# Reciprocals on GpSimd, a second place for context rows, and earlier norms of tile 1, in a layer of windowed attention and a ternary feed-forward

## The chip, the cores and the metric

The kernel is one program that runs on all 8 cores of one Trainium2 chip. Each core has five engines with instruction streams of their own: PE (TensorE, matrix products and transposes into PSUM), DVE (VectorE), ACT (ScalarE), POOL (GpSimd) and SP (SyncE, which here only starts DMAs). They meet only in semaphores. The metric is device time in microseconds of the slowest of the 8 cores. The cores get different rows of the input and the same weights.

## The reference, cut to what matters

```python
x = x + _layernorm(attn(_layernorm(x), Wq, Wk, Wv, Wo))     # attention over 4 sinks and the last 512 keys
x = x + _layernorm(ffn(_layernorm(x), fast_b, w_fc, w_proj, u, v, gate))

def _bitlinear(x, w_latent):
    scale = clip(mean(abs(w_latent), axis=1, keepdims=True), 1e-05, None)
    tern = clip(round(w_latent / scale), -1.0, 1.0)
    w = w_latent + stop_gradient(tern - w_latent)
    return x @ (w * scale).T
h = _bitlinear(x, w_fc) + gate * (x @ v.T @ fast_b.T @ u.T)   # w_fc: 4096 x 1024
r = maximum(h, 0.0)
return _bitlinear(r * r, w_proj)                              # w_proj: 1024 x 4096
```

`x` is 2 x 16384 x 1024. The mask leaves attention only to the last 516 rows of each batch entry; all other rows pass through the feed-forward part alone. Each core has 4096 rows.

## The kernel before, in words

**Tiles.** The 4096 rows of a core are 8 tiles of 512 rows, and a tile is 4 blocks of 128 rows (i = 0 to 31). A block is normed (`stats1`, `apply1` on DVE, `rstd1` on ACT between them), transposed into `xnT`, multiplied in 32 chunks of hidden units (`fc(j, hc)` into the three PSUM banks `fcb`), put through ReLU (`relu`, ACT, makes `rpp`) and squared (`square`), and multiplied by the second weight (`proj`). From tile 2 on all squares are DVE's.

**Preparation.** Both weights are made ternary on the core while tiles 0 and 1 pass. There are 64 units of 128 x 1024: 32 of `w_fc` (n = 0 to 31) and 32 of `w_proj` (n = 32 to 63). A unit is loaded (`wload` on SP, into one of nine places, so unit n + 9 mostly follows unit n), its absolute values are summed (`abssum`, ACT), and for every four units POOL makes a threshold (`group`, writes `thr`, `hsc2`, `nthr`). `cut(n)` on DVE compares in two passes, `below` and `tern` (`ternp` for `w_proj`), and a DMA turns the result into `Sfc` or `Spj`. For a quarter of the first 32 units (`BY_PE`) PE turns it instead (`unit`) and ACT copies it out of the PSUM tile `pt` (`evac`). The low-rank term is folded into the same comparison: POOL scales `us` by the reciprocal `rthr` of the threshold into `usd`, `ut(g)` on PE turns it into `pt`, ACT copies it (`ut_copy`), and `low_rank(n)` multiplies into PSUM, where `cut(n)` reads it.

**Order.** Each engine runs a loop of its own over n = 0 to 63 that is written out by hand. In iteration n DVE cuts unit n + 2, PE does `fc(0, n - 2)` and `low_rank(n + 3)`, and ACT does `abssum(n + 8)` and the ReLU of chunk n - 3. The reciprocals are `over(g)` on DVE, in the iterations 4, 8 and so on ahead of `cut(n + 2)`. The four blocks of tile 1 are loaded after units 11, 13, 15 and 17 (`XROWS`) and normed in the iterations 25 to 28 (`STATS`). In iteration 33 PE turns the four blocks, ACT copies them (`turned`), and tile 1's 32 chunks follow (`CHUNKS`), with first halves of tile 0's products among them. `out_scale(0)` on PE stands behind the turns and in front of tile 1's chunks.

**Context rows.** In tile 2 the 645 rows of attention's context (six groups, the last of 5 rows) are normed between chunks: `ln(g)` after chunk 4g + 3, `ln_end(g)` after chunk 4g + 4. They are loaded through POOL's queue into the one tile `lrow`, so that the load of group g waits for `ln_end(g - 1)`. The same queue loads the attention's weights into two tiles `wsl`.

## Time and profile before

| | before |
|---|---|
| median of 3 runs | 1085.4 us (1084.92 to 1088.9) |
| profiled execution: its own time | 1083.28 us |
| profiled execution: span of the slowest core (core 5) | 1081.7 us |
| spans of the 8 cores | 1075.2 to 1081.7 us |
| PE busy | 1004.2 us, 93% of the span |
| DVE, ACT, POOL busy | 52%, 34%, 4% |
| DMA read from HBM, written | 87.79 MB, 17.31 MB |

The span runs from the first to the last instruction of the slowest core; the execution's own time is 1.6 us longer. PE is near its limit over the whole, so what can change is in the stretches in which it is not. All rows below are of core 5, and times in them count from the start of its span.

### The profile page before, as it was taken

Reading aid. Unit: us, or ns where it says so; the run is one execution under the profiler, and the core shown is the slowest. Engines: PE = TensorE matmul, PEld = TensorE weight load, DVE = VectorE, ACT = ScalarE, POOL = GpSimd, SP = SyncE. Lnnn points to the kernel's source line nnn. Section 1 sums busy time; section 2 is a strip of 40 time slices with the busy share of each in tenths; the row PEclk is TensorE's granted clock in tenths of the full one; section 3 lists DMA queues with packets and bytes.
Section 4 is the critical chain, followed back from the end, with each engine's and each line's share of the span. In section 5 each row is a group of like instructions: output and inputs, shape, how many; then the busy total and the mean of one; then the engine's idle time right before and its main releaser. Section 6 shows DMA issues by size and latency. Waiting matters only on the chain.

```text
span 1081.7 us, 14983 instructions; the slowest of 8 cores (1075.2 to 1081.7 us)
## 1 busy us (share of the span) xinstructions
PE 1004.2 (93%) x4933; PEld 456.6 (42%) x4933; DVE 563.5 (52%) x819; ACT 362.6 (34%) x699; POOL 39.0 (4%) x97
## 2 busy tenths in 40 slices
PE   3789769999999789999999999999999999999997
PEld 1223234444444334544544444445444444444443
DVE  4878968735555443553445344634445354544333
ACT  4779787530003431134211341123301232013200
POOL 0001011000001000000000000000000000000000
PEclk9999889999999999999999999999999999999999
DMA  8899788923553214610445123622244301311011
GB/s 268 191 241 292 188 223 204 219 60 107 146 137 102 72 37 108 162 51 8 75 108 128 47 45 78 156 59 65 46 109 138 78 21 30 113 54 40 1 64 54
DMA packets 106367, 116.93 MB, mean 108 GB/s; under 512 B 82333, under 2 KB 82589, under 8 KB 106292
## 3 DMA queue, kind: packets, MB, share of 16 engines
q1 hardware_dynamic: 102324, 103.64, 36.9%
q0 software_dynamic: 3728, 12.25, 5.9%
q8 instruction: 42, 0.69, 0.3%
q14 instruction: 33, 0.27, 0.1%
q10 hardware_dynamic: 240, 0.07, 0.0%
HBM read 87.79 MB, written 17.31 MB: 97 GB/s over the span
## 4 chain that ended last, share of the span: by engine, by line
PE 78%; DMA 7%; DVE 6%; issue 5%; ACT 3%; SPq 1%; POOL 0%; DVEq 0%; ACTq 0%; POOLq 0%
PE pjp L642 37%; PE fcb L625 28%; PE pjp L625 2%; DMA lrow<-ctx 2%; DMA Sfc<-tern 1%; PE xp L788 1%; PE xp L642 1%; PE xp L751 1%; PE fcb L642 1%; ACT rpp L1019 1%; DVE below L1426 1%; DMA r<-x 1%; DMA stg<-wpj 1%; PE pt L625 1%; ACT absd L1059 1%
## 5 line engine op out<-in xcount | busy, mean ns | idle before, releaser
L625 PE MATMUL fcb<-xnT,Sfc 128*128 128x512 bf16 x1792 | 405.8, 383 | 17.0 <-DVE r L1402 14.4
L642 PE MATMUL pjp<-Spj,r 128*128 128x512 fp8e4 x1664 | 366.8, 380 | 1.7 <-DVE r2b L1402 1.7
L625 PEld LDWEIGHTS fcb<-xnT,Sfc 128*128 128x128 bf16 x1792 | 171.7, 99 | 234.0 <-issue 42.4
L1402 DVE TENSOR_TENSOR r<-fcb,rpp 128x512 bf16<-128x512 f32 x192 | 131.2, 689 | 225.4 <-ACT rpp L1019 225.3
L642 PEld LDWEIGHTS pjp<-Spj,r 128*128 128x128 bf16 x1664 | 161.0, 98 | 195.7 <-issue 7.2
L1019 ACT ACTIVATE rpp<-fcb,hsc 128x512 f32<-128x512 f32 x192 | 130.3, 686 | 209.1 <-PE fcb L625 199.4
L982 ACT ACTIVATE lv<-mv,cvecs 128x1 f32<-128x1 f32 x64 | 18.8, 293 | 288.4 <-DVE mv L1356 206.4
L1346 DVE TENSOR_TENSOR xy<-pjp,oscb 128x512 f32<-128x512 f32 x60 | 41.3, 688 | 133.0 <-PE pjp L642 133.0
L642 PE MATMUL pjp<-Spj,r2b 128*128 128x512 fp8e4 x256 | 55.4, 379 | 0.0
L1351 DVE BATCH_NORM_STATS2 s<-xy 128x6 f32<-128x512 f32 x64 | 44.4, 694 | 9.4 <-DVE xy L1346 6.1
L625 PE MATMUL pjp<-xnT,Sfc 128*128 128x512 bf16 x176 | 42.2, 392 | 0.0
L1368 DVE TENSOR_TENSOR xy<-xy 128x1024 f32<-128x1024 f32 x31 | 37.9, 1223 | 4.3 <-DVE xy L1360 4.3
L1059 ACT ACTIVATE absd<-xy 128x1024 fp8e4<-128x1024 f32 x32 | 33.6, 1051 | 14.6 <-DMA xy<-wpj 7.4
L642 PEld LDWEIGHTS pjp<-Spj,r2b 128*128 128x128 bf16 x256 | 25.0, 98 | 30.2
L1360 DVE TENSOR_SCALAR xy<-xy,mv,rs 128x1024 f32<-128x1024 f32 x31 | 25.1, 810 | 16.6 <-ACT rs L983 16.6
L1129 ACT ACTIVATE Pb<-Sm,nmx 128x516 bf16<-128x516 f32 x16 | 11.6, 725 | 66.1 <-DVE nmx L1477 62.0
L1326 DVE TENSOR_SCALAR xn<-xs,mv,rs 128x1024 bf16<-128x1024 f32 x26 | 21.1, 812 | 21.1 <-ACT rs L983 21.0
L625 PEld LDWEIGHTS pjp<-xnT,Sfc 128*128 128x128 bf16 x176 | 17.8, 101 | 22.0 <-issue 2.7
L1313 DVE BATCH_NORM_STATS2 st<-xs 128x6 f32<-128x512 f32 x26 | 17.9, 687 | 9.9 <-DMA xs<-x 9.9
L1019 ACT ACTIVATE rpp<-fcb,thr 128x512 f32<-128x512 f32 x32 | 21.4, 670 | 0.0
L1059 ACT ACTIVATE absd<-stg 128x1024 fp8e4<-128x1024 f32 x18 | 18.9, 1051 | 7.5 <-DMA stg<-wpj 6.5
L1438 DVE SCALAR_TENSOR_TENSOR ternp<-xy,thr,below 128x1024 fp8e4<-128x1024 f32 x16 | 20.6, 1285 | 1.7
(176 smaller groups left out, 681.2 us busy)
## 6 DMA issues: line engine op xcount, KB each, us to landing
xy<-x SPq DMA_DIRECT2D x31, 512.0 KB, 4.6
out<-xy SPq DMA_DIRECT2D x31, 512.0 KB, 3.0
xs<-x SPq DMA_DIRECT2D x25, 512.0 KB, 5.1
xy<-wfc SPq DMA_DIRECT2D x16, 512.0 KB, 5.9
xy<-wpj SPq DMA_DIRECT2D x16, 512.0 KB, 5.0
stg<-wfc SPq DMA_DIRECT2D x10, 512.0 KB, 6.4
stg<-wpj SPq DMA_DIRECT2D x8, 512.0 KB, 5.2
xs<-wpj SPq DMA_DIRECT2D x8, 512.0 KB, 5.1
```

Source lines behind the costliest of these rows:

```text
L625: mm = te.matmul(bank, s_fc[:, dci * HF + hc * 128:dci * HF + hc * 128 + 128], xnT[:, dci * TT:(dci + 1) * TT], start=(dci == 0), stop=(dc ...
L642: mm = te.matmul(dst, squares(j)[:, hc * TT + s * 128: hc * TT + s * 128 + 128], spj_even[:, hc // 2, hc % 2, half * 512:half * 512 + 512] ...
L982: settled(sc.activation(tmp, var, AF.Ln, bias=eps_p[0:n, :]))
L1019: sc.activation(rpp[n % 2][:], bank, AF.Relu, scale=scale[:, hc:hc + 1]).then_inc(a_rl, 1)
L1059: sc.activation(absd[:], stg[SLOT[n]][:], AF.Abs, accum_out=wsum[:, n:n + 1], saturate=False).then_inc(a_abs, 1)
L1326: ve.tensor_scalar(xn_of(i), rows1(i), mv1[:, 2 * i:2 * i + 1], rs1[:, i:i + 1], ALU.subtract, ALU.mult).then_inc(v_xn, 1)
L1346: ve.tensor_tensor(yy[i % 2][:, cols], src, oscb[:, cols], ALU.mult).then_inc(v_y, 1)
L1351: ve.bn_stats(s2[:, 6 * half:6 * half + 6], yy[i % 2][:, cols]).then_inc(v_st, 1)
L1360: settled(ve.tensor_scalar(yy[i % 2][:], yy[i % 2][:], mv2[:, 2 * i:2 * i + 1], rs2[:, i:i + 1], ALU.subtract, ALU.mult))
L1368: ve.tensor_tensor(yy[i % 2][:], yy[i % 2][:], xr[i % 2][:], ALU.add).then_inc(v_out, 1)
L1402: ve.tensor_tensor(squares(j)[:, hc * TT:(hc + 1) * TT], bank, rpp[n % 2][:], ALU.mult).then_inc(v_r2, 1)
L1438: ve.scalar_tensor_tensor(dst, stg[SLOT[n]][:], thr[:, c:c + 1], below[n % 2][:], ALU.is_gt, ALU.subtract, saturate=sat).then_inc(v_ab, 1)
```

## The change

It has six parts, on all engines:

- The reciprocal of the threshold is made by POOL as a power with exponent -1 (column 5 of `cvec`, spread over four columns), in front of the scaling of `us`. `over` and its semaphore go, on DVE.
- `BY_PE` are the units 3, 7 and so on to 31, where it was 2, 6 and so on to 30. PE waits before a unit for the eviction of the one before.
- Tile 1's blocks are loaded after the units 6, 10, 14 and 18, and normed in the iterations 12, 16, 20 and 24.
- Of their four transposes ACT copies two, and DVE two (`turned` on DVE, at the head of iteration 34).
- In the iterations 30 to 34 ACT does ReLU and square of tile 0's chunk before the sum of a unit, and `out_scale(0)` waits for the ReLU of 30 chunks, where it was 32.
- Context rows have a second place, which is the tile `wsl1`. Group g's load waits for `ln_end(g - 2)`, and the first query weights, which use the same tile, are loaded when all six groups are normed.

```diff
-XROWS = {11: 0, 13: 1, 15: 2, 17: 3}
+XROWS = {6: 0, 10: 1, 14: 2, 18: 3}
-BY_PE = [n for n in range(NFU) if n % 4 == 2]
+BY_PE = [n for n in range(NFU) if n % 4 == 3]
+EVAC = {n: k + 1 for k, n in enumerate(BY_PE)}
-STATS = {25: 4, 26: 5, 27: 6, 28: 7}
+STATS = {12: 4, 16: 5, 20: 6, 24: 7}
+        crow = [lrow[:], wsl[1][:].bitcast(F32)]
             def rows(g):
-                if g > 0:
-                    gp.wait_ge(v_lnr, g)
-                gp.dma_start(lrow[0:GROWS[g], :],
+                if g > 1:
+                    gp.wait_ge(v_lnr, g - 1)
+                gp.dma_start(crow[g % 2][0:GROWS[g], :],
...
+                    settled(gp.tensor_tensor(rthr[:, c], thr[:, c],
+                                             cvec[:, 5:6].broadcast_to(
+                                                 (128, GRP)), ALU.pow))
                     if g > 1:
                         gp.wait_ge(p_ut, g - 1)
-                    gp.wait_ge(v_rt, g + 1)
...
             rows(0)
+            rows(1)
             gp.dma_start(mask[:], t_mw[:, :]).then_inc(d_msk, 16)
             gp.dma_start(msB[:], t_ms[:, :]).then_inc(d_msk, 16)
-            rows(1)
             weights(0, piece(t_wk, 0))
-            rows(2)
+            for g in range(2, NG):
+                rows(g)
+            gp.wait_ge(v_lnr, NG)
             weights(1, piece(t_wq, 0))
-            for g in range(3, NG):
-                rows(g)
...
                 if j == 1:
-                    te.wait_ge(a_xt, 2 * NSUB)
+                    te.wait_ge(a_xt, NSUB + 2)
+                    te.wait_ge(v_xt, 2)
...
                 if q == 0:
                     te.wait_ge(d_idf, 16)
-                    te.wait_ge(a_rl, HCN)
+                    te.wait_ge(a_rl, HCN - 2)
...
                 if n == HCN + 1:
-                    for i in range(NSUB, 2 * NSUB):
-                        turned(i)
+                    turned(NSUB)
+                    turned(NSUB + 1)
...
+                if HCN - 2 <= n < HCN + 3:
+                    relu(0, n - 3)
+                    square(0, n - 3)
                 for u in SUMS[n]:
                     abssum(u)
...
-            def over(g):
-
-                c = slice(GRP * g, GRP * g + GRP)
-                ve.wait_ge(g_thr, g + 1)
-                ve.reciprocal(rthr[:, c], thr[:, c]).then_inc(v_rt, 1)
...
             for n in range(NUNIT):
-                if n > 1 and n % GRP == 0 and n + 4 < NFU:
-                    over(n // GRP + 1)
+                if n == HCN + 2:
+                    turned(NSUB + 2)
+                    turned(NSUB + 3)
```

The order of instructions on DVE, in the program around the norms of tile 1, is before (`below` and `tern` are one cut, `st`, `mv` and `xn` are one norm, and `rthr` is the reciprocal):

```order
L1410 RECIPROCAL rthr<-thr 128x4
L1426 SCALAR_TENSOR_TENSOR below<-xs,nthr,xp 128x1024
L1438 SCALAR_TENSOR_TENSOR tern<-xs,thr,below 128x1024
L1313 BN_STATS st<-Spj 128x6
L1314 BN_STATS st<-Spj 128x6
L1315 BN_AGGR mv<-st 128x2
L1426 SCALAR_TENSOR_TENSOR below<-xy,nthr,pjp 128x1024
L1438 SCALAR_TENSOR_TENSOR tern<-xy,thr,below 128x1024
L1313 BN_STATS st<-Spj 128x6
L1314 BN_STATS st<-Spj 128x6
L1315 BN_AGGR mv<-st 128x2
L1326 TENSOR_SCALAR xn<-Spj,mv,rs 128x1024
```

and in the changed kernel, from the first of these norms, two cuts before iteration 12:

```order
L1327 BN_STATS st<-Spj 128x6
L1328 BN_STATS st<-Spj 128x6
L1329 BN_AGGR mv<-st 128x2
L1443 SCALAR_TENSOR_TENSOR below<-stg,nthr,xp 128x1024
L1455 SCALAR_TENSOR_TENSOR tern<-stg,thr,below 128x1024
L1340 TENSOR_SCALAR xn<-Spj,mv,rs 128x1024
L1443 SCALAR_TENSOR_TENSOR below<-stg,nthr,pjp 128x1024
L1455 SCALAR_TENSOR_TENSOR tern<-stg,thr,below 128x1024
L1443 SCALAR_TENSOR_TENSOR below<-xs,nthr,xp 128x1024
L1455 SCALAR_TENSOR_TENSOR tern<-xs,thr,below 128x1024
L1443 SCALAR_TENSOR_TENSOR below<-xs,nthr,pjp 128x1024
L1455 SCALAR_TENSOR_TENSOR tern<-xs,thr,below 128x1024
```

The four norms stood one behind each of the cuts 26 to 29 and stand now one to every four cuts, from cut 13 on; no reciprocal is left among them.

On ACT, around the turned blocks of tile 1 (`absd` is the sum of a unit, `rpp` and `r` are ReLU and square of a chunk, `xnT` the turned blocks), before:

```order
L1059 ACTIVATE absd,wsum<-stg 128x1024
L1019 ACTIVATE rpp<-fcb,thr 128x512
L1037 ACTIVATE r<-rpp 128x512
L999 ACTIVATE xnT<-pjp 128x8x128 x2
L999 ACTIVATE xnT<-pt 128x8x128
L999 ACTIVATE xnT<-xp 128x8x128
L1059 ACTIVATE absd,wsum<-stg 128x1024
L1019 ACTIVATE rpp<-fcb,thr 128x512
L1037 ACTIVATE r<-rpp 128x512
L1059 ACTIVATE absd,wsum<-stg 128x1024
L1019 ACTIVATE rpp<-fcb,thr 128x512
L1037 ACTIVATE r<-rpp 128x512
```

and in the changed kernel:

```order
L1030 ACTIVATE rpp<-fcb,thr 128x512
L1048 ACTIVATE r<-rpp 128x512
L1070 ACTIVATE absd,wsum<-stg 128x1024
L1010 ACTIVATE xnT<-pjp 128x8x128 x2
L1030 ACTIVATE rpp<-fcb,thr 128x512
L1048 ACTIVATE r<-rpp 128x512
L1070 ACTIVATE absd,wsum<-stg 128x1024
L1030 ACTIVATE rpp<-fcb,thr 128x512
L1048 ACTIVATE r<-rpp 128x512
L1070 ACTIVATE absd,wsum<-stg 128x1024
```

The ReLU of chunk 29, for which `out_scale(0)` waits now, stands ahead of the sum and of the turned blocks; the ReLU of chunk 31, for which it waited, stood behind all of them.

POOL's queue at the context rows, before:

```order
L489 DMA lrow<-ctx 128x1024
L548 DMA mask<-mw 128x516
L549 DMA msB<-ms 16x4
L489 DMA lrow<-ctx 128x1024
L495 DMA wsl<-wk 128x2048
L489 DMA lrow<-ctx 128x1024
L495 DMA wsl<-wq 128x2048
```

and in the changed kernel:

```order
L492 DMA lrow<-ctx 128x1024
L492 DMA wsl<-ctx 128x1024
L555 DMA mask<-mw 128x516
L556 DMA msB<-ms 16x4
L498 DMA wsl<-wk 128x2048
L492 DMA lrow<-ctx 128x1024
L492 DMA wsl<-ctx 128x1024
L492 DMA lrow<-ctx 128x1024
L492 DMA wsl<-ctx 5x1024
L498 DMA wsl<-wq 128x2048
```

Odd groups go to `wsl`, and the query weights moved behind the last group.

## Rows read from the trace of the kernel before

**Rows 1.** The page: slices of the span (40 equal parts of 27 us).

```profile
PE 3789769999999789999999999999999999999997
```

**Rows 2.** Windows: stretch, busy us of PE, PEld, DVE, ACT, POOL, clock, DMA.

```profile
39.40:133.10 93.70, 78.93 (x366) 29.31 (x365) 79.05 (x79) 75.52 (x133) 8.18 (x28) 0.93 0.97 239
133.10:150.50 17.40, 8.67 (x62) 4.97 (x61) 15.06 (x17) 14.78 (x25) 2.90 (x4) 0.79 0.92 241
150.50:241.20 90.70, 86.74 (x401) 40.24 (x399) 58.83 (x66) 54.65 (x92) 9.59 (x24) 0.98 0.70 166
338.90:394.90 56.00, 43.65 (x228) 19.99 (x226) 28.68 (x49) 22.08 (x40) 3.76 (x7) 1.00 0.26 71
```

**Rows 3.** Waits of DVE, 39 to 133 us: us in total, times, longest.

```profile
DVE rthr L1410 <- POOL nthr L516: 4.7, 5, 1.3
DVE below L1426 <- PE xp L688: 2.7, 2, 2.4
DVE below L1426 <- DMA Sfc<-tern: 1.8, 1, 1.8
DVE below L1426 <- PE pjp L688: 1.7, 1, 1.7
```

**Rows 4.** Timeline of DVE: start, us, operation, idle before. Cuts and a norm.

```profile
38.72 1.28 DVE L1426 SCALAR_TENSOR_TENSOR below<-stg,nthr,xp 128x1024 bf16<-128x1024 f32 x1 [0.28 <-PE xp L688]
...
50.90 1.27 DVE L1426 SCALAR_TENSOR_TENSOR below<-xs,nthr,xp 128x1024 bf16<-128x1024 f32 x1
...
53.48 1.27 DVE L1426 SCALAR_TENSOR_TENSOR below<-xy,nthr,pjp 128x1024 bf16<-128x1024 f32 x1
...
62.88 1.27 DVE L1426 SCALAR_TENSOR_TENSOR below<-xy,nthr,xp 128x1024 bf16<-128x1024 f32 x1
...
120.08 0.69 DVE L1313 BATCH_NORM_STATS2 st<-Spj 128x6 f32<-128x512 f32 x1
...
122.36 1.27 DVE L1426 SCALAR_TENSOR_TENSOR below<-xy,nthr,pjp 128x1024 bf16<-128x1024 f32 x1
...
131.83 1.28 DVE L1438 SCALAR_TENSOR_TENSOR tern<-stg,thr,below 128x1024 bf16<-128x1024 f32 x1
```

**Rows 5.** POOL's groups of instructions: line, shapes, count, busy us, mean ns, idle before.

```profile
L533 POOL TENSOR_TENSOR thr<-wsum 128x1 f32<-128x1 f32 x8 | 4.7, 590 | 1.1
...
L521 POOL TENSOR_TENSOR usd<-us,rthr 128x64 bf16<-128x64 f32 x8 | 2.3, 292 | 5.1 <-DVE rthr L1410 5.1
...
L514 POOL TENSOR_TENSOR hsc<-thr 128x4 f32<-128x4 f32 x8 | 1.6, 200 | 1.2
```

**Rows 6.** Timeline of ACT, DVE and PE, 139 to 241 us.

```profile
142.03 1.92 ACT L999 ACTIVATE xnT<-pjp 128x1024 bf16<-128x1024 bf16 x2
...
154.25 0.69 ACT L1019 ACTIVATE rpp<-pjp,thr 128x512 f32<-128x512 f32 x1 [0.29 <-PE pjp L625]
...
142.57 0.75 DVE L1432 TENSOR_SCALAR below<-xy,nthr 128x1024 bf16<-128x1024 f32 x1 [0.15 <-DVE ternp L1438]
...
157.15 0.69 DVE L1402 TENSOR_TENSOR r2b<-pjp,rpp 128x512 bf16<-128x512 f32 x1 [5.84 <-ACT rpp L1019]
...
149.97 0.77 PE L715 MATMUL fcb<-identf,thr 128*128 128x128 f32 x2 [8.73 <-ACT rpp L1019]
...
183.13 1.89 PE L642 MATMUL xp<-Spj,r 128*128 128x512 fp8e4 x8 [2.23 <-DMA Spj<-ternp]
```

**Rows 7.** The page's DMA issues: KB each, us from issue to landing.

```profile
xy<-wpj SPq DMA_DIRECT2D x16, 512.0 KB, 5.0
```

**Rows 8.** Timeline of PE in tile 2's chunks, with the idle time before.

```profile
354.21 1.89 PE L625 MATMUL fcb<-xnT,Sfc 128*128 128x512 bf16 x8 [3.27 <-DVE r L1402]
...
393.10 1.89 PE L625 MATMUL fcb<-xnT,Sfc 128*128 128x512 bf16 x8 [0.60 <-DVE r L1402]
```

**Rows 9.** Waits of PE in 338.9 to 394.9 us, and of DVE in 326 to 400 us.

```profile
PE fcb L625 <- DVE r L1402: 12.4, 6, 3.3
...
DVE ast L1447 <- DMA lrow<-ctx: 8.5, 4, 2.3
```

More of the change, by code:

```diff
@@ L263, in build_nc @@
         d_out = [sem("d_out0"), sem("d_out1")]
-        d_row = sem("d_row")
+        d_row = [sem("d_row0"), sem("d_row1")]
         d_msk = sem("d_msk")
@@ L277, in build_nc @@
         g_us = sem("g_us")
-        v_rt = sem("v_rt")
         g_own = sem("g_own")
@@ L326, in build_nc @@
         a_xt = sem("a_xt")
+        v_xt = sem("v_xt")
         v_y = sem("v_y")
@@ L485, in rows @@
             def rows(g):
-                if g > 0:
-                    gp.wait_ge(v_lnr, g)
-                gp.dma_start(lrow[0:GROWS[g], :],
+                if g > 1:
+                    gp.wait_ge(v_lnr, g - 1)
+                gp.dma_start(crow[g % 2][0:GROWS[g], :],
                              t_ctx[g * 128:g * 128 + GROWS[g], :]
-                             ).then_inc(d_row, 16)
+                             ).then_inc(d_row[g % 2], 16)
             def weights(m, src):
@@ L543, in _ @@
             gp.wait_ge(d_us, 16)
+            gp.wait_ge(d_cv, 16)
             for g in range((NFU + NPU) // GRP):
@@ L595, in unit_in @@
                 if n in BY_PE:
-                    te.wait_ge(a_ev, n // 4 + 1)
+                    te.wait_ge(a_ev, EVAC[n])
                 else:
@@ L671, in ut @@
                     te.wait_ge(a_ut, g)
-                if g > 1:
-                    te.wait_ge(a_ev, g - 1)
+                last = [m for m in BY_PE if m <= max(1, GRP * (g - 1))]
+                if g > 0 and last:
+                    te.wait_ge(a_ev, EVAC[last[-1]])
                 for k in range(GRP):
@@ L699, in unit @@
                 te.wait_ge(v_ab, n + 1)
-                te.wait_ge(a_ut, min(n // GRP + 2, NFU // GRP))
+                te.wait_ge(a_ut, min(n // GRP + 2 if n > 1 else 1,
+                                     NFU // GRP))
+                if EVAC[n] > 1:
+                    te.wait_ge(a_ev, EVAC[n] - 1)
                 for blk in range(DCN):
@@ L1047, in evac @@
             def evac(n):
-                sc.wait_ge(p_un, n // 4 + 1)
+                sc.wait_ge(p_un, EVAC[n])
                 sc.activation(sfc3[:, :, n * 128:n * 128 + 128],
@@ L1244, in _ @@
                     out_scale(0)
-                if 3 <= n < HCN + 3:
+                if 3 <= n < HCN - 2:
                     relu(0, n - 3)
@@ L1369, in plus_x, with turned @@
                                  ALU.add).then_inc(v_out, 1)
+            def turned(i):
+                s = i % NSUB
+                ve.wait_ge(p_xt, i + 1)
+                ve.tensor_copy(xnT3[:, :, s * 128:s * 128 + 128],
+                               turn_bank(i).rearrange("p (c t) -> p c t",
+                                                      t=128)
+                               ).then_inc(v_xt, 1)
             def last_rows(i):
@@ L1397, in square @@
                         if k in BY_PE:
-                            ve.wait_ge(p_un, k // 4 + 1)
+                            ve.wait_ge(p_un, EVAC[k])
                         else:
@@ L1418, in cut @@
                 if n - 3 in BY_PE:
-                    ve.wait_ge(p_un, n // 4 + (n % 4 > 2))
+                    ve.wait_ge(p_un, EVAC[n - 3])
                 elif n > 2:
@@ L1455, in ln @@
                     ve.memset(QB[:], 0.0).then_inc(v_zero, 1)
-                ve.wait_ge(d_row, 16 * (g + 1))
-                stats(g, lrow[0:n, :])
+                ve.wait_ge(d_row[g % 2], 16 * (g // 2 + 1))
+                stats(g, crow[g % 2][0:n, :])
             def ln_end(g):
@@ L1463, in ln_end @@
                     ve.wait_ge(p_lt, g)
-                ve.tensor_scalar(lnb[0:n, :], lrow[0:n, :],
+                ve.tensor_scalar(lnb[0:n, :], crow[g % 2][0:n, :],
                                  amv[0:n, 2 * g:2 * g + 1],
@@ L1552, in _ @@
             apply1(2)
-            over(0)
             stats1(3)
@@ L1565, in _ @@
                     cut(n + 2)
-                if n == 0:
-                    over(1)
                 if n + 1 in STATS:
```

## The prediction, on record before the changed kernel ran

> **What bounds the kernel now.** I read the slices of the page first, to see where PE is not full. It is full from about 240 us on, with one dip in slices 13 and 14 (the 56.0 us below), and has its larger gaps in the first six slices [rows 1]. The windows then give the size of each: in the 93.7 us from 39.4 to 133.1 PE works 78.9 and DVE 79.1; in the 17.4 us behind it PE works 8.7, at a clock of 0.79; from 150.5 to 241.2 it lacks 4.0; and in the dip of 56.0 us it lacks 12.35 [rows 2]. These four stretches are the whole of what the change can move.
>
> In the first stretch I go by DVE, since each unit must pass through its cut. A cut is 2.58 us from one start to the next (50.90 to 53.48) and a norm of tile 1 is 2.28 (120.08 to 122.36) [rows 4]. The 28 cuts from 38.72 and the four norms are 28 x 2.58 + 4 x 2.28 = 81.4 us. The last cut ends at 131.83 + 1.28 = 133.1, so 94.4 us went by, and 13.0 of them were something else: 4.7 of waiting in front of reciprocals, 4.4 for PE's low-rank products, 1.8 for a tern buffer whose transpose had not landed [rows 3], and the reciprocals and hand-overs themselves. I call the end of the last cut Z; it is 133.1 now, and all later events of the preparation hang on it.
>
> **The change, part by part: up to Z.** Half of the gain should lie here. In the iterations 4, 8 and so on the reciprocal makes DVE wait for the next group's threshold two cuts before a cut needs it. Without it DVE first needs that group through the low-rank product of cut 4g + 3, one cut later. The norms go from where DVE had no other slack (cuts 27 to 30, 4.86 us each) to the middle. There a group of four cuts and a norm is 4 x 2.58 + 2.28 = 12.6 us of DVE. ACT has for the same group about 75.5 / 93.7 of the time [rows 2], and PE less, so DVE becomes the engine that never waits, and the waits of 1.3 us and less disappear under the norm.
>
> The price is a longer way from the sum of a unit to `usd`. The power has no row here. Its bounds are 0.20 us (the product of 128x4 on POOL) and 1.28 (the longest instruction of DVE or POOL in the chain); I take 0.7, between them, and nearer to the mean of 0.59 that a POOL instruction takes when DVE is at work [rows 5]. POOL now idles 5.1 / 8 = 0.64 us in front of `usd`, for the reciprocal; the power and a hand-over of 1.1 / 8 = 0.14 [rows 5] take 0.84, so the chain gets 0.2 longer, and 0.3 where the reciprocal was prompt. In addition `evac` of unit 4k + 3 (about 1.0 us, like the copies of turned blocks [rows 6]) stands in ACT's queue directly ahead of the sum that ends a group, where before it stood one unit earlier. And POOL's instructions now run while DVE cuts: two instructions of the chain at 0.59 in place of 0.20 are 0.8 more [rows 5]. Together some 2.1 us per group. In a group with a norm the norm's 2.3 us cover them. Before cut 12 they stand against the wait of 1.3 and the reciprocal of 0.2 that go, so cut 12, now at 62.88 [rows 4], starts at 62.88 - 1.5 + 2.1 = 63.5.
>
> A rule of the Trainium skill bears on this (SBUF — State Buffer, the section with the two separate sides): VectorE and GpSimd have a port pair in common that one of them locks for a whole instruction, and a VectorE instruction with two SBUF inputs locks out a GpSimd instruction that reads SBUF. The second pass of a cut is one of these. By that rule the trace agrees as far as it goes (means of 0.59 against 0.20). If every one of the five instructions of the chain were held for a whole pass, the sum of the preparation would lose its gain; by the rows it is 0.4 for some.
>
> The four loads of tile 1's rows fell into seven units before and now come one to four units, each just ahead of a unit whose transpose is PE's; the DMA share in the stretch is 0.97 [rows 2], so transfers can hold up something wherever they are. I leave half of the waits for PE and for transposes standing, (4.4 + 1.8) / 2, less 0.8 for the half of the 1.7 [rows 3] that lies before cut 12: 2.3 us.
>
> Z after = 63.5 + 16 x 2.58 + 4 x 2.28 + 4 x 2.58 + 2.3 = 126.5. **Gain 6.6 us**, bounds: 0 (chain and DMA take all of it) and 13 (all waits gone).
>
> **Behind Z.** PE waits 8.73 us at 149.97 for the ReLU of chunk 31 before `out_scale(0)` [rows 6]. That wait goes: ReLU 29 is done when the turns are, ACT copies two blocks (1.92), DVE two. The copy on DVE has no row; the nearest are 1.0 (ACT, same shape) and the bounds 0.69 (half the width) and 1.28 (a cut's pass). I take 1.05, so 2.1 us of DVE in front of cut 36. PE then starts tile 1 some 7 us nearer to Z. But what is late next is not PE. The fourth chunk needs the ReLU of the first one, and in ACT's queue that stands behind the sum of unit 45, which takes the place of unit 36. Now: ReLU at 154.25, that is Z + 21.1, and the first square on DVE at 157.15, Z + 24.0 [rows 6]. After: cut 36 starts at 142.57 - 133.1 + 2.1 = Z + 11.5 or so and ends at Z + 13.5, the load is issued 1.3 later and lands in 5.0 [rows 7], the sum is 1.1: ReLU at Z + 21, the second chunk's ReLU 1.3 later, square at Z + 23.1. DVE cuts on from there, and PE waits for unit 47 at 183.13 as before (now 2.23, then more). **Gain 0.9 us** of the 8.7: most is given back as a wait of PE for the first ReLU and for unit 47. Bounds: -1.5 (copies of 1.28, a load of 6) and +4 (ACT is not behind its loads). From unit 47 on PE is full in both kernels, until 241.
>
> **Context rows.** Behind chunks 8, 12, 16 and 20 PE waits together 11.5 us, and behind the group of 5 rows, for whose load DVE hardly waits, 0.60 [rows 8, 9]. DVE waits 8.5 us for the four loads [rows 9]. With two places a load is issued seven chunks (12 us) before its use and lands in about 5 [rows 7]. So each of the four waits goes to 0.60: 12.4 of PE's wait becomes 0.24 + 5 x 0.60 = 3.2. **Gain 9.1 us**, bounds 7 and 11. It has no cover that could hide it: PE is full from there to the end. The query weights now come behind the last group; they are needed two halves of a product (2 x 6.9 us) and more later, so they cost nothing; if they came late it would be at most a load, 5 us. DVE's norms, POOL's issues and ACT's copies are the same in number.
>
> **Sum.** 6.6 + 0.9 + 9.1 = 16.6 us. The profiled execution took 1083.3 (a span of 1081.7 and 1.6 around it) and would take 1066.7; the median of the runs is 2.1 higher, 1085.4, and gives 1068.8. I say 1069.
>
> **Rivals.**
> - *Preparation gains nothing* (DMA at a share of 0.97 sets the pace, or the longer chain through POOL does, or PE's clock falls in the small gaps that each norm makes, as the 0.79 behind Z shows it can, and PE becomes the late one). For it: if each of the five POOL instructions is held for a whole second pass of a cut, 5 x 1.28 = 6.4 us stand against 2.3 of slack in a group. Against it: DVE's and DMA's work are spread, not raised. Time: 1085.4 - 9.1 = 1076. Chance 0.22.
> - *More than the sum*: all 13.0 us of waits go: 1068.8 - (13.0 - 6.6) = 1062, and with ACT ahead of its loads 1060. Chance 0.10.
> - *Context rows gain nothing*, since DVE then waits for something else, say the transposes through PSUM: 1085.4 - 7.5 = 1078. Against it: the 0.60 of the last group, which has the same steps. Chance 0.04.
> - *Slower than before*: the power on POOL is no short instruction. It is in series with each of the eight groups. Above 0.7 each us costs one per group where no slack is left, so from 16.6 / 8 + 0.7 = 2.8 us on the gain is gone; at 5 us, the time is 1085.4 + 8 x 2.2 = 1103. Against it: nothing on POOL took over 1.28 here. Chance 0.04.
> - *The forecast*, 1063 to 1073: chance 0.60.
>
> **How the numbers follow.** The range is 1060 to 1077: it takes in the forecast, the larger gain and nearly all of the first rival, and leaves out the slower one and the edge of the others. About 0.5% (5.4 us, from 1080 to 1091) is what a measurement can tell from no change. Faster by more than that are all cases but the slow one and the tails: 0.93; within 0.03; slower 0.04.
>
> **What the profile would show.** Right: the last cut of `w_fc` ends near 126.5; DVE has no wait above 1 us between cuts 12 and 28; POOL's power is under 1.3 us; PE's wait for the scales is gone, and one of 3 to 6 us stands instead in tile 1's first chunks, for a ReLU; the wait for unit 47 is longer than 2.23; the waits of PE for DVE in tile 2's chunks are 3 us together, and no wait for a context load is left on DVE. Wrong: waits of PE for `usd` that grew above 1.4 each, a clock well under 0.93 before Z, or waits for `lrow` and `wsl`.

## The result, and the profile after

| | before | after |
|---|---|---|
| median of the runs | 1085.4 us (1088.9 over the runs beside those of after) | 1076.2 us |
| ratio after / before, with its 95% interval | 1 | 0.991 (0.9891 to 0.993) |
| profiled execution: its own time | 1083.28 us | 1073.45 us |
| its spans over the 8 cores | 1075.2 to 1081.7 us | 1067.5 to 1071.9 us |

The 1088.9 and the five executions of after hold some in which one die ran slower at a lower clock; the ratio leaves these out. The change makes the kernel 0.9% faster, some 9.8 us. The 1076.2 lies in the range that was given, 1060 to 1077, but at its edge; 16.6 us were forecast, and 1069. All rows of after below are of core 2, the slowest one.

The waits of PE in tile 2's chunks, 338.9 to 394.9 us (us in total, times, longest), and tile 1's first chunks on PE, with the two copies on DVE ahead of them, show the parts that went as forecast or nearly so:

```profile
PE fcb L632 <- DVE r L1425: 3.1, 6, 0.6
```

```profile
146.42 0.69 DVE L1389 COPY xnT<-pt 128x1024 bf16<-128x1024 bf16 x1 [0.47 <-PE pt L595]
147.03 0.68 DVE L1389 COPY xnT<-xp 128x1024 bf16<-128x1024 bf16 x1
...
147.86 3.61 PE L632 MATMUL pjp<-xnT,Sfc 128*128 128x512 bf16 x16 [0.82 <-DVE xnT L1389]
...
157.87 5.30 PE L632 MATMUL pjp<-xnT,Sfc 128*128 128x512 bf16 x16 [4.67 <-ACT rpp L1030]
```

The first row answers to the 12.4 of [rows 9]: 9.3 us are gone. The second fence answers to the 8.73 of [rows 6]: tile 1's first chunk starts 147.86 - 134.6 = 13.3 us behind Z where it was 17.4 [rows 2], and three chunks later PE waits 4.67 for the first ReLU. Z is the end of the last cut of `w_fc`, as in the prediction, and it is what went wrong. DVE's timeline:

```profile
61.51 1.28 DVE L1455 SCALAR_TENSOR_TENSOR tern<-xy,thr,below 128x1024 bf16<-128x1024 f32 x1
66.64 1.28 DVE L1443 SCALAR_TENSOR_TENSOR below<-xy,nthr,pjp 128x1024 bf16<-128x1024 f32 x1 [3.85 <-PE pjp L696]
...
70.41 1.28 DVE L1443 SCALAR_TENSOR_TENSOR below<-xy,nthr,xp 128x1024 bf16<-128x1024 f32 x1 [1.10 <-PE xp L696]
...
133.30 1.28 DVE L1455 SCALAR_TENSOR_TENSOR tern<-stg,thr,below 128x1024 bf16<-128x1024 f32 x1
```

Cut 12 starts at 70.41 where 63.5 was forecast, and Z is 134.6 where 126.5 was. From cut 12 to Z are 64.2 us; the forecast had 63.0. So 6.9 of the 8.1 us by which Z is missed on this core lie *before* cut 12, in the three groups that have no norm. There DVE waits for low-rank products (3.85 us ahead of cut 11), and PE, which makes them, stood behind `ut`, which waits for POOL's `usd`. POOL's timeline for the groups 1 and 3, and DVE's pass beside the first of them:

```profile
34.65 0.23 POOL L519 TENSOR_SCALAR nthr<-thr 128x4 f32<-128x4 f32 x1
34.84 1.04 POOL L521 TENSOR_TENSOR rthr<-thr,cvecs 128x4 f32<-128x4 f32 x1
36.02 1.35 POOL L526 TENSOR_TENSOR usd<-us,rthr 128x64 bf16<-128x64 f32 x1
...
61.72 1.16 POOL L515 TENSOR_SCALAR thr<-wsum 128x4 f32<-128x4 f32 x1 [11.44 <-ACT absd L1070]
63.03 0.20 POOL L517 TENSOR_TENSOR hsc<-thr 128x4 f32<-128x4 f32 x1
63.20 0.23 POOL L519 TENSOR_SCALAR nthr<-thr 128x4 f32<-128x4 f32 x1
63.39 1.03 POOL L521 TENSOR_TENSOR rthr<-thr,cvecs 128x4 f32<-128x4 f32 x1
64.63 0.29 POOL L526 TENSOR_TENSOR usd<-us,rthr 128x64 bf16<-128x64 f32 x1 [0.20 <-POOL rthr L521]
```

```profile
35.94 1.28 DVE L1455 SCALAR_TENSOR_TENSOR tern<-xy,thr,below 128x1024 bf16<-128x1024 f32 x1 [0.51 <-DVE below L1443]
```

The power takes 1.03 us and its hand-over to `usd` 0.20. `usd`, which starts 0.08 us behind DVE's pass, takes 1.35 us in place of 0.29 and ends 0.15 behind it; the `thr` at 61.72 likewise stretches over the pass from 61.51 (1.16 in place of 0.23 to 0.28). On PE (timeline, idle time before in brackets) this is:

```profile
37.74 0.59 PE L684 MATMUL pt<-identb,usd 128*16 128x128 bf16 x4 [5.42 <-POOL usd L526]
...
40.20 3.59 PE L632 MATMUL fcb<-xnT,Sfc 128*128 128x512 bf16 x8
...
45.51 3.55 PE L632 MATMUL fcb<-xnT,Sfc 128*128 128x512 bf16 x8
...
49.53 1.90 PE L632 MATMUL fcb<-xnT,Sfc 128*128 128x512 bf16 x8
...
65.38 0.38 PE L684 MATMUL pt<-identb,usd 128*16 128x128 bf16 x4 [3.72 <-POOL usd L526]
65.70 0.84 PE L696 MATMUL pjp<-gfold,uTs 16*128 16x512 bf16 x2
66.47 3.30 PE L632 MATMUL fcb<-xnT,Sfc 128*128 128x512 bf16 x8
```

Behind the gap of 5.42 us two chunks take 3.6 us each, where a chunk at the full clock takes 1.90: the clock is at its lower level of 1.2 GHz for them. Behind the 3.72 it is one chunk, with 3.30. The length of the gap alone doesn't decide it: over the cores one or two chunks are long behind the same 5.42, and on core 2 two are behind a gap of 2.21 and none behind one of 2.22, in the groups with a norm, where DVE then waits again (1.21 us ahead of cut 24, 1.69 ahead of cut 25):

```profile
103.58 0.58 PE L684 MATMUL pt<-identb,usd 128*16 128x128 bf16 x4 [2.21 <-POOL usd L526]
...
105.06 3.59 PE L632 MATMUL fcb<-xnT,Sfc 128*128 128x512 bf16 x8
...
109.55 3.59 PE L632 MATMUL fcb<-xnT,Sfc 128*128 128x512 bf16 x8
```

```profile
109.72 1.28 DVE L1443 SCALAR_TENSOR_TENSOR below<-stg,nthr,xp 128x1024 bf16<-128x1024 f32 x1 [1.21 <-PE xp L696]
...
114.08 1.28 DVE L1443 SCALAR_TENSOR_TENSOR below<-xs,nthr,pjp 128x1024 bf16<-128x1024 f32 x1 [1.69 <-PE pjp L696]
```

In the profile of before the gap at the place of the 5.42 was 3.63 us (at 36.08), and only one chunk behind it was long (3.07). PE's waits for `usd` from 20 to 140 us (total, times, longest) are in before and in after:

```profile
PE pt L676 <- POOL usd L521: 13.7, 7, 4.3
```

```profile
PE pt L684 <- POOL usd L526: 19.6, 7, 5.4
```

Since one core is not a kernel, the experiments go by the median over all eight cores of the profiled execution. Each number is read from the timelines of the cores: start of the second pass of cuts 4 and 12, Z, the start of tile 1's second product (from there on PE is full in every kernel, so I call it the end of the preparation), and PE's waits for `usd` from 20 to 140 us.

```
                       cut 4  cut 12   Z      end    usd   ratio  (95% interval)
before                  39.4   63.9  131.9   239.5  12.9  1
after                   42.1   69.3  133.6   240.2  20.0  0.991  (0.9891-0.993)
context rows alone      39.8   63.9  132.3   240.2  12.8  0.9914 (0.9898-0.993)
 and norms spread       39.5   65.4  128.1   236.2  15.2  0.9876 (0.9853-0.99)
after, DVE's reciprocal
  at its old place      39.5   66.9  130.0   236.8  16.3  0.9882 (0.9864-0.9899)
  and units 2, 6, ..    39.5   64.6  125.7   233.9  14.6  0.985  (0.9832-0.9869)
  one cut later         39.6   67.9  145.7   253.6  26.9  1.0051 (1.0037-1.0065)
after, units 2, 6, ..   42.1   67.5  129.8   235.9  18.1  0.9914 (0.99-0.9928)
  and the power first   40.7   65.8  126.7   234.1  15.5  0.9883 (0.9865-0.9902)
after, a product in the
  power's place         39.2   66.0  127.7   234.7  13.8  0.987  (0.9856-0.9884)
  and units 2, 6, ..    39.5   64.0  125.2   232.2  12.5  0.9836 (0.9821-0.985)
after, PE filled, start 41.7   69.5  131.6   238.8  14.9  0.9915 (0.9898-0.9932)
  and at each group     41.6   69.5  132.2   239.8  10.1  0.992  (0.9907-0.9934)
DVE's reciprocal, units
  2, 6, .. and filled   39.2   63.0  124.0   231.4   7.1  0.9845 (0.9825-0.9865)
```

How far such a median scatters, the kernels show whose programs are the same up to Z. Before and the context rows alone have 131.9 and 132.3. The spread norms (128.1) and DVE's reciprocal with units 2, 6, .. (125.7) differ, up to Z, in nothing but a wait of PE for an eviction four units back. So a single step of Z of 2 or 3 us shows little by itself.

### The profile page after: what moved, and what is told of

The parts are those of the page before. It is cut to its first block, busy times and chain, and to the rows that moved or that the text cites. A ratio compares the mean times of both kernels' runs of the same rounds, so it can differ in the third digit from the quotient of the medians.

```text
span 1071.9 us, 14984 instructions; the slowest of 8 cores (1067.5 to 1071.9 us)
## 1 busy us (share of the span) xinstructions
PE 1007.4 (94%) x4933; PEld 455.6 (43%) x4933; DVE 562.9 (53%) x813; ACT 361.5 (34%) x697; POOL 48.6 (5%) x105
## 4 chain that ended last, share of the span: by engine, by line
PE 82%; DVE 5%; issue 4%; DMA 4%; ACT 2%; POOL 1%; SPq 1%; ACTq 0%; DVEq 0%; POOLq 0%
PE pjp L649 38%; PE fcb L632 31%; PE pjp L632 2%; PE xp L799 1%; PE xp L649 1%; PE xp L762 1%; PE fcb L649 1%; DVE below L1443 1%; ACT rpp L1030 1%; PE pt L632 1%; DMA r<-v 1%; DMA Sfc<-tern 1%; ACT absd L1070 1%; PE pjp L696 1%; POOL rthr L521 1%
## 5 line engine op out<-in xcount | busy, mean ns | idle before, releaser
L632 PE MATMUL fcb<-xnT,Sfc 128*128 128x512 bf16 x1792 | 410.0, 386 | 8.1 <-DVE r L1425 4.9
L1374 DVE TENSOR_SCALAR xy<-xy,mv,rs 128x1024 f32<-128x1024 f32 x31 | 25.1, 811 | 16.6 <-ACT rs L994 16.6
L632 PEld LDWEIGHTS pjp<-xnT,Sfc 128*128 128x128 bf16 x176 | 17.4, 100 | 28.6 <-issue 9.7
L684 PE MATMUL pt<-identb,usd 128*16 128x128 bf16 x32 | 3.7, 249 | 19.6 <-POOL usd L526 19.6
L1455 DVE SCALAR_TENSOR_TENSOR tern<-xy,thr,below 128x1024 bf16<-128x1024 f32 x16 | 20.5, 1284 | 2.1 <-DVE below L1443 0.5
```

Of the source, the lines that this page charges most:

```text
L632: mm = te.matmul(bank, s_fc[:, dci * HF + hc * 128:dci * HF + hc * 128 + 128], xnT[:, dci * TT:(dci + 1) * TT], start=(dci == 0), stop=(dc ...
L1374: settled(ve.tensor_scalar(yy[i % 2][:], yy[i % 2][:], mv2[:, 2 * i:2 * i + 1], rs2[:, i:i + 1], ALU.subtract, ALU.mult))
L1455: ve.scalar_tensor_tensor(dst, stg[SLOT[n]][:], thr[:, c:c + 1], below[n % 2][:], ALU.is_gt, ALU.subtract, saturate=sat).then_inc(v_ab, 1)
```

## The experiments

**Where does the measured gain come from?** Before, with the edit of the context rows alone.

```diff
+        crow = [lrow[:], wsl[1][:].bitcast(F32)]
...
-                if g > 0:
-                    gp.wait_ge(v_lnr, g)
-                gp.dma_start(lrow[0:GROWS[g], :],
+                if g > 1:
+                    gp.wait_ge(v_lnr, g - 1)
+                gp.dma_start(crow[g % 2][0:GROWS[g], :],
```

> The kernel before with the context rows' second place alone (odd groups in the weight tile, the query weights behind the last group). If all of the measured gain is the context rows, as the two traces suggest (PE's wait for DVE's squares in tile 2 fell from 12.4 to about 3 us, while the end of the preparation stayed), this takes 9 to 10 us less than before: a ratio of 0.991 to 0.992, the same as the changed kernel. If the preparation's edits gained something too and the context rows less, the ratio is 0.995 or more.

Measured: 0.9914 (0.9898 to 0.993), and after is 0.991. The waits of [rows 9] are 3.4 us in this kernel. So the context rows give 9.3 us, the forecast was 9.1, and the five other parts of the change together give nothing that can be told from zero.

**The norms.** The same kernel, with the loads and norms of tile 1 spread over the groups.

```diff
-XROWS = {11: 0, 13: 1, 15: 2, 17: 3}
+XROWS = {6: 0, 10: 1, 14: 2, 18: 3}
-STATS = {25: 4, 26: 5, 27: 6, 28: 7}
+STATS = {12: 4, 16: 5, 20: 6, 24: 7}
```

> The kernel before with the context rows' second place, and with tile 1's loads and norms spread as in the change; reciprocals on DVE, PE's units at 2, 6 and so on, and the turned blocks as before. Against the context rows alone (0.9914): if the spread of the norms is worth what the prediction said, it takes 5 us or more off (0.987), and the last cut of the first weight ends near 126 us. If the loads disturb the other transfers as much as the norms are hidden, it is within 2 us of them.

Measured: 0.9876 against 0.9914, so 0.38% or 4.1 us (the two intervals just meet), and Z is 132.3 - 128.1 = 4.2 us earlier; by the means of the two pairs with the same program up to Z it is 132.1 - 126.9 = 5.2. The spread norms do most of what was argued. DMA does not set the pace here, though its share is as high as before (0.98 from 39.4 to 128 us), so that reason of the first rival falls.

**The power's length.** After, with a product of the same shape on POOL in the power's place. The reciprocals, and with them the low-rank part, have wrong values.

```diff
                     settled(gp.tensor_tensor(rthr[:, c], thr[:, c],
                                              cvec[:, 5:6].broadcast_to(
-                                                 (128, GRP)), ALU.pow))
+                                                 (128, GRP)), ALU.mult))
```

> The changed kernel with a product in place of the power on POOL (the reciprocals are then wrong values, and so is the low-rank term; every instruction, shape and wait is the same). If the 1.04 us of the power on the way from a group's sums to its low-rank products is what ate the preparation's gain, the power's row falls from 1.03 to about 0.2, cut 4 starts 0.9 to 1.7 us earlier and cut 12 3 us or more, and the kernel is 3 to 6 us faster than the changed one. If the place of PE's units and the eviction ahead of the sum is the cause, it is at most 1 us faster, and PE's waits for usd stay near their 19.6 us in total.

The groups of POOL (count, busy us, mean ns) in after and with the product:

```profile
L521 POOL TENSOR_TENSOR rthr<-thr,cvecs 128x4 f32<-128x4 f32 x8 | 8.3, 1032 | 0.0
```

```profile
L521 POOL TENSOR_TENSOR rthr<-thr,cvecs 128x4 f32<-128x4 f32 x8 | 1.6, 198 | 0.0
```

The operation alone makes 0.83 us of difference in each of the eight groups, 6.7 us together. Z comes 5.9 us earlier and the time falls by 0.4%, 4.3 us. In the first group more than the 0.83 goes: `usd` takes 0.29 us on all eight cores, where after has 1.35 or 1.36 on all eight, and PE's first wait for it is 3.51 in place of 5.42.

**The units that PE turns.** After, with the units 2, 6 and so on again.

```diff
-BY_PE = [n for n in range(NFU) if n % 4 == 3]
+BY_PE = [n for n in range(NFU) if n % 4 == 2]
```

> The changed kernel with the units that PE turns back at 2, 6 and so on to 30. If the cause is that the eviction now stands directly ahead of the sum that closes a group, and that PE has no work between the first low-rank product and its first chunk, cut 12 starts 3 us or more earlier, PE's waits for usd fall from 19.6 to about 14 us in total, and the kernel is 3 to 5 us faster than the changed one. If the power is the cause it is within 1.5 us of the changed one.

Measured: Z 3.8 us earlier and the end of the preparation 4.3 us, but the time is the same as after's. The median core gains, the slowest does not (means over the four runs: 1067.8 in place of 1071.0, and 1074.3 in place of 1074.1): the spans of the profiled execution go from 1063.4 to 1076.1 us, where after's went from 1067.5 to 1071.9. A long span goes with a low granted clock:

```profile
core 4: 1064.0 us, clock 0.994
core 5: 1076.1 us, clock 0.983
```

Over the 32 spans of the four runs that this kernel's ratio rests on, span and clock have a correlation of -0.90. In the other changed kernels it lies between -0.39 and -0.90. This says that chunks at the lower clock and late cores come together, not which makes which.

**Reciprocals back on DVE.** After, with `over` on DVE at its old place (and its semaphore), first with units 3, 7 and so on, then with 2, 6 and so on.

```diff
-                    settled(gp.tensor_tensor(rthr[:, c], thr[:, c],
-                                             cvec[:, 5:6].broadcast_to(
-                                                 (128, GRP)), ALU.pow))
+                    gp.wait_ge(v_rt, g + 1)
...
+                if n > 1 and n % GRP == 0 and n + 4 < NFU:
+                    over(n // GRP + 1)
```

> The changed kernel with the reciprocals back on DVE at their old place, PE's units at 3, 7 and so on as in the change. If the eviction directly ahead of a group's last sum matters, it is 2 to 4 us slower than the same kernel with the units at 2; if the units' place is free, within 1 us of it. By the power's theory it is 3 to 5 us faster than the changed kernel.

> The changed kernel with the reciprocals back on DVE at their old place, and PE's units back at 2, 6 and so on: norms, turned blocks on two engines, scales and context rows as in the change. If the way through POOL is what ate the gain, the last cut ends near 126 us, PE's waits for usd are about 13 us in total and it is 8 us or more faster than the changed kernel (0.983). If DVE's wait in front of the reciprocal costs as much as the power, it is within 2 us of the run with a product for the power (0.987).

Measured: 0.9882 and 0.985. The second kernel is the change without its power and without its new choice of units. Its Z is 125.7 and its median 1068.6 us, where the prediction had 126.5 and 1069. And with a prompt reciprocal on DVE `usd` is never held: it takes 0.29 or 0.30 us in every group of every core, as in before, since it starts right behind the reciprocal, at least 1.1 us ahead of the second pass of DVE's next cut. The difference between the two, units alone, is 4.3 us of Z and 0.32% of the time; the difference between the first and after, the power alone, is 3.6 us of Z and 0.28%. Each of these two steps of the time is within touching intervals and rests on Z as well; both together, 0.985 against 0.991, are clear, and so is the power with units 2, 6 and so on, 0.64% and 4.1 us of Z (0.9914 against 0.985).

**A late reciprocal on DVE.** The same, with `over` one cut later, so that DVE hardly waits for a threshold.

```diff
                     cut(n + 2)
+                if n == 0 or (n % GRP == 0 and n + 4 < NFU):
+                    over(n // GRP + 1)
```

> The changed kernel with the reciprocal back on DVE, but one cut later than in the kernel before (in the iterations 0, 4, 8 and so on behind the cut, not ahead of it), and no power on POOL. If the power's 1.04 us is the cause, the chain is shorter by 0.6 to 0.9 us a group except where DVE comes late to the reciprocal, and the kernel is 2 to 5 us faster than the changed one. If the units' place is the cause, it is within 1.5 us. If DVE comes late with the reciprocal in the groups with a norm, PE's waits name the usd of POOL behind DVE's rthr, and it is slower.

Measured: 1.0051, slower than *before*, and 1.7% or 18 us above the kernel with `over` at its old place (0.9882), from which it differs in order alone. DVE's waits, 39 to 145 us:

```profile
DVE below L1448 <- PE pjp L695: 18.4, 10, 2.4
DVE below L1448 <- PE xp L695: 9.9, 8, 2.2
```

The threshold comes while DVE is in a cut; the reciprocal then stands up to two passes behind it (from the start of the threshold to the end of `usd` it is 5.3 us in the groups 4 to 6, where the old place has 1.7 to 2.1), PE's `ut` waits for it (26.9 us in all), and DVE pays it back at once as a wait for the low-rank products behind `ut`, 28.3 us. With `over` at its old place (its slowest core, the same window) it waits 3.6 for them and 4.3 for thresholds. So the early wait of DVE was cheap and useful: it bought a prompt reciprocal. Taking it away is worth something only if the reciprocal stays as prompt.

**What would a free reciprocal on POOL be worth?** After, with the product in the power's place and units 2, 6 and so on (wrong low-rank values again; both edits are shown above).

> The changed kernel with a product in place of the power (wrong reciprocals, same instructions and waits) and PE's units back at 2, 6 and so on. With the product alone it was 0.987, with the units alone 0.9914, with both edits undone through DVE's reciprocal 0.985. If DVE's early wait for the threshold costs nothing, this is 0.985 as well; if that wait was worth removing, as the change and the prediction had it, this is 0.983 or less.

Measured: 0.9836, against 0.985 with DVE's reciprocals. The intervals overlap: moving the reciprocal off DVE is worth 0.14%, 1.5 us, if anything, even if it cost POOL only 0.20 us.

**The order on POOL.** Units 2, 6 and so on, and the power ahead of the two short instructions, with the wait for its end behind them.

```diff
+                    own[0] += 1
+                    gp.tensor_tensor(rthr[:, c], thr[:, c],
+                                     cvec[:, 5:6].broadcast_to((128, GRP)),
+                                     ALU.pow).then_inc(g_own, 1)
                     gp.tensor_tensor(hsc2[:, c], thr[:, c], thr[:, c],
...
+                    gp.wait_ge(g_own, own[0])
```

> The changed kernel with PE's units back at 2, 6 and so on, and with the power started on POOL as soon as the threshold is there, ahead of the square and the negated threshold. The way to usd is shorter by some 0.4 us a group than in the changed kernel. If the length of that way times the low clock behind each long gap is the cause, it is 2 us or more faster than the changed kernel with the units moved back alone (0.9914), and the first wait for usd after the start falls from 5.4 to about 5.0 us, or further if POOL is not held by DVE's cut. If not, it is the same.

POOL and DVE in the first group, on core 5, with the power last and with the power first:

```profile
36.84 1.35 POOL L526 TENSOR_TENSOR usd<-us,rthr 128x64 bf16<-128x64 f32 x1
...
36.75 1.28 DVE L1455 SCALAR_TENSOR_TENSOR tern<-xy,thr,below 128x1024 bf16<-128x1024 f32 x1 [0.51 <-DVE below L1443]
```

```profile
35.71 0.29 POOL L528 TENSOR_TENSOR usd<-us,rthr 128x64 bf16<-128x64 f32 x1
...
35.79 1.29 DVE L1457 SCALAR_TENSOR_TENSOR tern<-xy,thr,below 128x1024 bf16<-128x1024 f32 x1 [0.51 <-DVE below L1445]
```

Measured: 0.9883 against 0.9914 of the kernel with the power last (the intervals just meet), cut 4 1.4 us earlier and Z 3.1. The two short instructions still stand ahead of `usd`, so the edit saves no more than a hand-over: `usd` starts 2.08 us behind the start of the threshold in place of 2.25. But 0.08 us ahead of DVE's pass it takes 0.29, and 0.09 behind its start 1.35, on all eight cores, and PE's first wait falls from 5.41 to 4.18. So in the first group the power costs 1.8 us of PE's wait (5.42 for 3.63), and 1.06 of them are the hold of `usd`, which comes from where it falls and not from its length.

**Is it PE's clock?** If the lower clock behind the gaps were what turns 1.8 us of longer chain at the first group into 5.4 at cut 12, work in the gaps should give it back. After, with ten products of 128x512 into a free PSUM bank ahead of the first `ut` of the loop, and then with four more ahead of each later one as well.

```diff
+                if n == 1:
+                    for k in range(10):
+                        te.matmul(fcb[2][:], identb[:], xnT[:, 0:TT],
+                                  start=True, stop=True)
+                elif n % GRP == 0 and 1 < n < NFU - 4 and 4:
+                    te.wait_ge(a_rl, max(n - 3, 0))
+                    for k in range(4):
...
```

> The changed kernel with ten extra 128x512 products of PE into a PSUM bank that nobody reads, in the idle time of 5.4 us before the second group's usd is turned. They add work and shorten no chain. If PE's clock, which is at its lower level when the first two chunks run behind that gap (3.6 us in place of 1.9), is what turns 1.7 us of a longer chain into 4 us at cut 8, the first chunks take 1.9 to 2.7 us, cut 8 starts 2 us or more earlier and the kernel is 1 to 4 us faster. If the chain alone matters, it is the same or slower.

> The same with four extra products also ahead of each later turn of usd, where PE waits 1 to 4 us. If the low clock behind these gaps is a part of the loss, the chunks of over 3 us go from 2 to 5 per core to 1 or none, and it is 1 to 3 us faster than the run with the extra products at the start alone. If not, it is the same; if the extra products hold up PE where usd was in time, it is slower.

PE in the first of these kernels (core 3, its slowest):

```profile
32.73 3.69 PE L947 MATMUL fcb<-xnT,identb 128*128 128x512 bf16 x10
38.24 0.38 PE L684 MATMUL pt<-identb,usd 128*16 128x128 bf16 x4 [1.82 <-POOL usd L526]
...
40.49 3.59 PE L632 MATMUL fcb<-xnT,Sfc 128*128 128x512 bf16 x8
```

Measured: 0.9915 and 0.992. The gap is 1.82 us in place of 5.42, and the chunk behind it still takes 3.59; over the cores it is 1.06 to 1.92, with one or two long chunks behind it on each. Z is 1.4 to 2.0 us earlier in the median core, and the time the same as after's. As a test of the clock it is inconclusive, since the chunks it was to make short stayed long.

A like filling in the best kernel (reciprocals on DVE, units 2, 6 and so on; eight products at the start and four at each group) did raise the clock.

> The best kernel so far (reciprocals on DVE at their old place, units at 2, 6 and so on, the rest as in the change; 0.985) with eight extra products at the start and four ahead of each later turn of usd. Its gaps are shorter (3.6 at the start, up to 2.4 later, one or two slow chunks a core). If the clock is a part of what is left, the last cut ends 1 to 3 us earlier and the ratio is 0.982 to 0.984; if the chain alone matters, it stays at 0.985 or is slower.

The window (stretch, busy us of PE, PEld, DVE, ACT, POOL, clock, DMA) on the slowest core, without the filling and with it:

```profile
30.00:140.00 110.00, 93.29 (x442) 35.54 (x440) 93.10 (x92) 89.68 (x157) 9.88 (x36) 0.94 0.99 238
```

```profile
30.00:140.00 110.00, 99.18 (x486) 38.71 (x485) 98.48 (x99) 93.22 (x164) 12.16 (x36) 0.98 1.05 251
```

Chunks of over 2.6 us up to Z are 2 on the eight cores together, where they were 19. The spans of the cores are 1058.8 to 1063.7 us at clocks of 0.992 to 0.997, and Z is 124.0, 1.7 us earlier. But the extra products take PE's time too (5.9 us more in the window), and the ratio is 0.9845 (0.9825 to 0.9865) against 0.985 (0.9832 to 0.9869): what the clock is worth there is below what these runs can tell.

## Why the prediction was right and wrong

- **Context rows: right.** 9.1 us forecast with bounds 7 and 11; 9.3 measured on this part alone. The wait of PE became 3.1, where 3.2 was worked out, as six short waits that the last group had shown [rows 8].
- **Behind Z: right on what is late next; the size is too small to be shown.** The end of the preparation lies 107.6 us behind Z before and 106.6 after (medians over the cores): 1.0, forecast 0.9. But single cores lie at 106.6 to 108.3 before and 105.1 to 108.3 after, so this agreement may be luck. PE's wait for the first ReLU is 4.67, forecast 3 to 6. Two details were off: the copy on DVE takes 0.69 and 0.68 us, the lower bound, not 1.05; and the wait for unit 47 did not grow above 2.23, it is 1.15 (0.7 to 1.9 over the cores, where before had up to 2.2).
- **Up to Z: wrong, and this is the miss.** The failed step is "cut 12 ... starts at 62.88 - 1.5 + 2.1 = 63.5". Two things are wrong in it. First, the price of 2.1 us per group was set against what goes *once*, but three groups pass before cut 12 and none has a norm beside it. The runs show the loss pile up: over the cores the cuts 4, 8 and 12 start 2.7, 4.2 and 5.4 us later than before, where 0.6 was forecast. Second, the power was taken at 0.7 us, inside bounds of 0.20 and 1.28; it takes 1.03, on top of which comes the hold of `usd` by DVE's pass (1.35 for 0.29) that was priced as a mean, though it falls on the first and least covered group, on every core. From the start of the threshold to the end of `usd` it is 3.6 us in group 1 and 3.0 in group 3, where before had 1.8 and 1.6 (medians over the cores); in the groups 4 to 7 it is 2.3, where before had 1.6 to 2.0.
- **From cut 12 to Z: nearly right.** 64.2 us on core 2 and 64.5 in the median, forecast 63.0. Yet the sign "DVE has no wait above 1 us between cuts 12 and 28" failed, with the 1.21 and 1.69 ahead of the cuts 24 and 25: the norms do not cover the chain in every group. Of the signs of being wrong, the waits of PE for `usd` above 1.4 showed (5.42, 3.72, 2.22 and 2.21 on core 2). A clock well under 0.93 did not (0.93 from 39.4 us to Z).
- **The price list of the chain, now from runs.** Units 3, 7 and so on cost 4.3 us of Z beside DVE's reciprocals and 3.8 beside the power: `evac` was priced at "about 1.0 us" per group and held to be covered; over seven groups it is some 0.6 each that isn't. The power costs 3.6 us of Z with the new units and 4.1 with the old ones. Without both, Z is 125.7; with both 133.6 = 125.7 + 4.3 + 3.6. They take back what the spread norms bring, 4.2 to 5.2 us of Z. The other edits (copies on two engines, ReLU ahead of the sums, the scales) stand behind cut 31 and cannot move Z. The end of the preparation is 240.2 in after and 240.2 with the context rows alone. In time: 0.985 + 0.0032 + 0.0028 = 0.991. Taken the other way round, the power is 0.0064 and the units nothing (0.9914 and 0.991), so only the sum of the two is settled.
- **Which rival came true.** "Preparation gains nothing", 1076 us, with a chance of 0.22, and of its three reasons the longer chain, through POOL and through the eviction ahead of the group's last sum. DMA was not it (norms spread: most of the gain at the same DMA share; and with the gaps filled DMA moved 251 GB/s from 30 to 140 us, where before moved 230). The clock comes behind the chain's gaps, but that it sets the time by itself was not shown: filling the gaps changed no time. What *against it* said, that work is spread and not raised, was true of DVE and beside the point, since the chain is latency. The 1076 was met within 0.2 us, and that the range held it, at its edge, is owed to this rival; the weight belonged more on it.
- **The rule of the Trainium skill** (SBUF — State Buffer, the two separate sides) that the prediction weighed: the trace agrees where a GpSimd instruction falls behind the start of DVE's two-input pass (1.35 for 0.29; 1.16 for 0.28), and where it starts ahead of the pass (0.29, in the kernel with the power first). It hit two of the five instructions in the first group (`thr` 0.55 to 0.56 and `usd` 1.35 to 1.36, on all eight cores) and in the later groups one, two or none. By the rule at its worst all five would have been held.

What stays open: why the kernel with units 2, 6 and so on and the power last ends its preparation 4.3 us earlier in the median core and is no faster in its slowest core. Its late cores have the lower clock; no run here separates cause and effect. It also wasn't tried to take the low-rank products of a group's last unit out from behind PE's wait for `usd`, which would uncouple DVE from the chain.

The best kernel found that computes the reference is the changed one with DVE's reciprocals where they were and units 2, 6 and so on: 1068.6 us, 0.985 of before.

## What to carry to other kernels

A wait on a busy engine can be what keeps a chain short. Before you move a small instruction off an engine because it "waits", follow who needs its result, and price the chain in *each* group in which nothing covers it, not once. Look also at what the moved instruction pushes the next one into: here a short `usd` slid behind the start of a pass on another engine and was held for all of it. And run a change of six parts in parts: here four of them gave 1.5% and two took back 0.6%, which the sum of all would never have shown.

## What the runs showed of the hardware

- A power on GpSimd over 128x4 float32 takes 1.03 us, a product of the same shape 0.20, the reciprocal on DVE 0.18 (1.4 us for eight, before).
- DVE copies 128x1024 bf16 from PSUM in 0.69 us, ACT in 0.97 (1.94 for two): the copy is cheaper than a pass of a cut (1.28), which was the prediction's upper bound.
- A GpSimd product over 128x64 took 0.29 us when it started 0.08 us ahead of a DVE pass with two SBUF inputs, and 1.35 when it started 0.09 us behind the pass's start.
- Behind a gap of 5.42 us two chunks ran at 1.2 GHz on four of the eight cores and one on the other four; on core 2 (3.59 and 3.55 us) there was one behind a gap of 3.72, two behind 2.21 and none behind 2.22. With ten products put into the first gap, and 1.06 to 1.92 us of idling left, one or two still ran slow on each core. In the kernel with the shorter chain eight products at the start left one of 2.94 us on one core and none on the others.
- Spans of the 8 cores of one execution differ by up to 12.7 us with the same program, the longer ones mostly at the lower clock (correlations of -0.39 to -0.90 in the changed kernels). The time is that of the slowest, so a gain of 4 us in the median core can be none.
